# A fused transformer layer on one core: two additions and one subtraction move to GpSimd, two accumulators swap banks, and pieces of the order on TensorE, VectorE and ScalarE change

## The reference, cut to what matters

```python
y = layernorm(x)
y = LN1(y + causal_attention(y, y, y))         # one head, d = 256
y = LN2(y + attention(y, ctx, ctx))            # 64 context rows
ff = relu(y @ w1 + b1) @ w2 + b2               # 256 -> 1024 -> 256
x1 = x + LN3(y + ff)
n  = fp4(layernorm(x1))                        # blocks of 16: scale, round to the FP4 grid
h  = silu(n @ w_gate.T) * (n @ w_up.T)         # 256 -> 704, weights in fp4 too
x2 = x1 + fp4(h) @ w_down.T                    # 704 -> 256
```

## Time and profile before

| | before |
|---|---|
| median of 3 runs | 654.59 us (651.49 to 655.66) |
| the profiled execution | 656.84 us, of it the span from first to last instruction 655.0 us |
| PE busy | 587.8 us (90%) |
| PEld, weight loads beside PE | 549.1 us (84%) |
| DVE busy | 517.7 us (79%) |
| ACT busy | 381.8 us (58%) |
| POOL busy | 345.7 us (53%) |
| mean granted clock of TensorE | 0.963 of full speed |

### The profile page before, as it was taken

The page is one execution under the profiler, slowest core; times in us unless marked ns, Lnnn a source line. Parts: engine busy times, 40 slices in busy tenths (PEclk is TensorE's granted clock), DMA queues, the critical chain, the costliest instruction groups (busy, mean ns, idle before and its releaser), DMA issues.

```text
span 655.0 us, 12390 instructions
## 1 busy us (share of the span) xinstructions
PE 587.8 (90%) x4021; PEld 549.1 (84%) x4021; DVE 517.7 (79%) x1268; ACT 381.8 (58%) x781; POOL 345.7 (53%) x416
## 2 busy tenths in 40 slices
PE   4876769999999999999999999999999998989665
PEld 3765759898989898998989898989899898988665
DVE  3688677788778878888879878887879877988752
ACT  3456365575747666666657574766666664746331
POOL 2555363574646655565547554655556554654521
PEclk9977898999999999999999999999999999999887
DMA  7601000010100101010101010010101000000000
GB/s 226 203 2 32 2 13 30 0 50 1 33 26 10 42 1 58 0 48 0 56 0 41 7 32 24 0 48 0 56 2 33 2 32 2 18 1 17 9 9 16
DMA packets 18743, 19.30 MB, mean 29 GB/s; under 512 B 1537, under 2 KB 18193, under 8 KB 18705
## 3 DMA queue, kind: packets, MB, share of 16 engines
q1 hardware_dynamic: 18704, 18.82, 9.3%
HBM read 14.62 MB, written 4.19 MB: 29 GB/s over the span
## 4 chain that ended last, share of the span: by engine, by line
PE 60%; DVE 20%; issue 9%; ACT 5%; POOL 2%; DMA 1%; SPq 1%; DVEq 0%; ACTq 0%; POOLq 0%
PE O L964 4%; PE R L983 4%; PE R L916 4%; PE TR L804 4%; PE R L918 4%; PE O L1008 4%; PE R L917 4%; PE O L1029 3%; PE O L1027 3%; PE O L1028 3%; PE R L984 3%; PE R L985 3%; PE R L804 3%; PE O L1009 3%; PE O L1010 3%
## 5 line engine op out<-in xcount | busy, mean ns | idle before, releaser
L453 POOL TENSOR_TENSOR rs<-mv,neg_half 128x1 f32<-128x1 f32 (+1 forms) x112 | 69.5, 626 | 53.2 <-DVE mv L1250 51.8
L916 PE MATMUL R<-gu_hi,xqT_hi 128*128 128x352 f32 x256 | 87.2, 341 | 3.2 <-issue 2.2
L459 POOL TENSOR_TENSOR hs<-hh,h_rec 128x704 f32<-128x704 f32 x32 | 44.6, 1393 | 76.5 <-DVE h_rec L1286 76.5
L983 PE MATMUL R<-y2T_hi,w_hi 128*128 128x256 f32 x256 | 78.4, 306 | 7.2 <-DVE y2T_lo L1383 5.0
L918 PE MATMUL R<-gu_hi,xqT_lo 128*128 128x352 f32 x256 | 83.9, 328 | 0.0
L917 PE MATMUL R<-gu_lo,xqT_hi 128*128 128x352 f32 x256 | 83.9, 328 | 0.0
L670 ACT ACTIVATE hqT_hi<-R 128x768 fp32r<-128x768 f32 x32 | 26.0, 813 | 92.0 <-PE R L804 92.0
L1027 PE MATMUL O<-w_hi,hT_hi 128*128 128x256 f32 x256 | 73.9, 289 | 0.0
L985 PE MATMUL R<-y2T_hi,w_lo 128*128 128x256 f32 x256 | 72.6, 284 | 0.0
L984 PE MATMUL R<-y2T_lo,w_hi 128*128 128x256 f32 x256 | 72.6, 283 | 0.0
L1029 PE MATMUL O<-w_hi,hT_lo 128*128 128x256 f32 x256 | 72.5, 283 | 0.0
(11 more groups left out here) (146 smaller groups left out, 1804.2 us busy)
## 6 DMA issues: line engine op xcount, KB each, us to landing
x_in<-in_x SPq DMA_DIRECT2D x16, 256.0 KB, 2.7
x_res<-in_x SPq DMA_DIRECT2D x16, 256.0 KB, 2.7
out<-x SPq DMA_DIRECT2D x32, 128.0 KB, 1.7
ctx_rows<-in_ctx SPq DMA_DIRECT2D x16, 64.0 KB, 2.4
hT<-in_L_xattn_w SPq DMA_DIRECT2D x1, 1024.0 KB, 8.1
hh<-in_L_xattn_w SPq DMA_DIRECT2D x1, 768.0 KB, 8.0
wd_raw<-in_L_ffn_w_down SPq DMA_DIRECT2D x1, 704.0 KB, 8.3
w_raw<-in_L_ffn_w_gate SPq DMA_DIRECT2D x1, 640.0 KB, 4.5
```

The lines of the kernel that those rows point to most:

```text
L916: mm(o, xh, gu_hi[:, c, m, cols], start=(c == 0), stop=False)
L983: mm(o, w1_hi[:, c, cols], y2T_hi[:, c, :], start=(c == 0), stop=False)
```

## The change

1. `x1_sum` for both tiles leaves VectorE and stands on GpSimd right behind `gamma3` of its tile.
2. The last lower half of relu(h), j = 3, becomes `h_lower_last` on GpSimd, behind `scale_h(0)`; the second piece of `ff2` waits for its own semaphore.
3. The banks of `values`, `down`, `down_add`, `self_reciprocal` and `self_sum` are swapped: tile t uses `O[t]`. `values(0)` thus waits for `cross_sum` only, and `values(1)` for `ff_sum(1)`. `ff2` for t = 0 now waits for both `down_add`, of which the second moves forward on VectorE.
4. On TensorE `ff2` for t = 1 is cut: its first quarter (the bias and six matmuls) runs ahead of `turn_hq(0)`.
5. VectorE: `h_scale(1)` and `h_reciprocal(1)` ahead of `cross_sum`; `shift(2)`, `hT_lower(0)` and `shift(3)` of tile 0 ahead of `ff_sum(1)` (the latter two were first in the next slot); `cross_max` ahead of `h_lift(0)`; `self_reciprocal(1)`, `self_sum(1)` earlier.
6. ScalarE: the upper half of y2 turned comes ahead of `norm_x`.

```diff
@@ -244,6 +245,7 @@
         FF2_CUT = 5 * FC // 8
+        FF2_TURN = FC // 4
         FIRST = 3
@@ -483,6 +485,11 @@
+def h_lower_last(b, h):
+    wait(pool, h_hi_set, b, h, F, 4, 4)
+    pool.tensor_tensor(hT_lo[:, 6:8, :], hT[:, 6:8, :], hT_hi[:, 6:8, :].bitcast(F32),
+                       ALU.subtract).then_inc(h_lo_last, 1)
+
 def residual(b, h):
@@ -504,6 +511,7 @@
         gamma3(b, g, 0)
+        x1_sum(b, g, 0)
     if q1:
@@ -511,6 +519,7 @@
         gamma3(b, g, 1)
+        x1_sum(b, g, 1)
         unscale_x(b, g, 0)
@@ -536,6 +545,8 @@
         scale_h(b, h, 0)
+    if f:
+        h_lower_last(b, h)
     if a:
@@ -557,6 +568,13 @@
     pool.tensor_tensor(z3[:, t, :], z3[:, t, :], g3_row[:], ALU.mult).then_inc(y3_set, 1)
+
+def x1_sum(b, h, t):
+
+    wait(pool, y3_set, b, h, F, T, t + 1)
+    wait(pool, xb_set, b, h, F, T, t + 1)
+    wait(pool, x2_set, b, h, Q + 1, T, t + 1)
+    pool.tensor_tensor(x1[(h - F) % 2][:, t, :], z3[:, t, :], xb[:, t, :], ALU.add).then_inc(x1_set, 1)
@@ -724,14 +742,14 @@
         norm(3, b, g, F, 0, T, z3[:, 0, :], z3[:, 0, :])
-    if front:
-        norm_x(b, h)
     if f:
         if isinstance(b, int) and HALVES * b + h == F:
             act.wait_ge(b1_fold_set, 1)
         wait(act, n2_turned, b, h, F, 1, 1)
         act.activation(y2T_hi[:], TR[1][:].rearrange("p (c r) -> p c r", c=KC),
                        ACT.Copy).then_inc(y2T_hi_set, 1)
+    if front:
+        norm_x(b, h)
     if q1:
@@ -951,9 +969,9 @@
             wait_batch(pe, exp_full, b, 1, 0)
+        wait(pe, z2_set, b, h, F, T, T)
+    else:
         wait(pe, z3_set, b, h, F + 1, T, T)
-    else:
-        wait(pe, z2_set, b, h, F, T, T)
     lhs = []
@@ -961,7 +979,7 @@
     for i, (key, e) in enumerate(lhs):
-        last = mm(O[1 - t][:, 0:D + 1], e, y0[:, key, :], start=(i == 0), stop=(i == len(lhs) - 1))
+        last = mm(O[t][:, 0:D + 1], e, y0[:, key, :], start=(i == 0), stop=(i == len(lhs) - 1))
     last.then_inc(pv_done, 1)
@@ -1001,7 +1019,7 @@
     wait(pe, z1_set, b, h, A - 1, T, t + 1)
-    o = O[1 - t][:, 0:D]
+    o = O[t][:, 0:D]
     for i in range(IC):
@@ -1014,9 +1032,11 @@
         wait(pe, h_hi_set, b, h, F, 4, n)
-        wait(pe, h_lo_set, b, h, F, 4, n)
+        wait(pe, h_lo_set, b, h, F, 3, min(n, 3))
+        if n == 4:
+            wait(pe, h_lo_last, b, h, F, 1, 1)
         if fs[0] == 0:
-            wait(pe, x2_set, b, h, Q + 1, T, 1)
+            wait(pe, x2_set, b, h, Q + 1, T, T)
     else:
@@ -1037,7 +1057,7 @@
         wait_batch(pe, ctx_lo_set, b, 1, 1)
-    wait(pe, x2_set, b, h, Q + 1, T, T)
+    wait(pe, x2_set, b, h, Q + 1, T, 1)
     for t in range(T):
@@ -1124,12 +1144,14 @@
         cross_values(b, h)
+    if f:
+        ff2(b, h, 1, range(FF2_TURN))
     if q:
         turn_hq(b, h, 0)
     if front and h == 0:
         turn_context(b)
     if f:
-        ff2(b, h, 1, range(FC))
+        ff2(b, h, 1, range(FF2_TURN, FC))
     prepare(b, h, "end")
@@ -1339,7 +1361,7 @@
     store_wait(b, h, t)
-    v.tensor_tensor(x2[:, t, :], O[1 - t][:, 0:D], x1[(h - Q) % 2][:, t, :], ALU.add).then_inc(x2_set, 1)
+    v.tensor_tensor(x2[:, t, :], O[t][:, 0:D], x1[(h - Q) % 2][:, t, :], ALU.add).then_inc(x2_set, 1)
@@ -1347,13 +1369,8 @@
     wait(dve, y2_set, b, h, F, T, t + 1)
+    wait(dve, x1_set, b, h, F + 1, T, t + 1)
     v.tensor_tensor(z3[:, t, :], O[1][:, 0:D], y2[t][:], ALU.add).then_inc(z3_set, 1)
-
-def x1_sum(b, h, t):
-    wait(dve, y3_set, b, h, F, T, t + 1)
-    wait(dve, xb_set, b, h, F, T, t + 1)
-    i = (h - F) % 2
-    v.tensor_tensor(x1[i][:, t, :], z3[:, t, :], xb[:, t, :], ALU.add).then_inc(x1_set, 1)
@@ -1427,10 +1444,6 @@
     prepare(b, h, "early")
-    if q1:
-        hT_lower(b, g, 0)
-    if f1:
-        shift(3, b, g, F, (0,))
     if a:
@@ -1441,11 +1454,14 @@
     if f1:
-        x1_sum(b, g, 0)
+        z3_stats(b, g, 1)
         x1_stats(b, g, 0)
+        aggregate(3, b, g, F, 1)
         aggregate(4, b, g, F, 0)
-        z3_stats(b, g, 1)
-        aggregate(3, b, g, F, 1)
+    if a:
+        self_reciprocal(b, h, 1)
+        self_sum(b, h, 1)
+    if f1:
         x_norm(b, g, 0)
@@ -1453,14 +1469,10 @@
         hT_lower(b, g, 1)
-    if a:
-        self_reciprocal(b, h, 1)
-        self_sum(b, h, 1)
     prepare(b, h, "self")
     if f1:
         x_lift(b, g, 0)
         x_drop(b, g, 0)
-        x1_sum(b, g, 1)
         x1_stats(b, g, 1)
@@ -1476,6 +1488,8 @@
         xT_lower(b, h, 0)
+    if q1:
+        down_add(b, g, 1)
     if f1:
@@ -1502,10 +1516,6 @@
         h_product(b, h, 1, 0)
-    if f:
-        h_lower(b, h, (3,))
-    if q1:
-        down_add(b, g, 1)
     if front:
@@ -1514,11 +1524,11 @@
         h_product(b, h, 1, 1)
-        h_lift(b, h, 0)
     if a:
         cross_max(b, h)
     prepare(b, h, "cross")
     if q:
+        h_lift(b, h, 0)
         h_drop(b, h, 0)
@@ -1526,12 +1536,12 @@
         ff_sum(b, h, 0)
-    prepare(b, h, "late")
-    if a:
-        cross_sum(b, h)
     if q:
         h_scale(b, h, 1)
         h_reciprocal(b, h, 1)
+    prepare(b, h, "late")
+    if a:
+        cross_sum(b, h)
     if a:
@@ -1542,11 +1552,15 @@
         aggregate(3, b, h, F, 0)
+    if a:
+        shift(2, b, h, A, (0, 1))
+    if q:
+        hT_lower(b, h, 0)
+    if f:
+        shift(3, b, h, F, (0,))
         ff_sum(b, h, 1)
     if front:
         shift(0, b, h + 1, 0, (0, 1))
-    if a:
-        shift(2, b, h, A, (0, 1))
     prepare(b, h, "end")
```

13 lines of the change are left out of this document (7 added, 6 removed).

## The result

The changed kernel takes **634.07 us** (median of 4 runs, 633.72 to 635.11); the kernel before, run beside it, 655.12 (651.49 to 656.72). The ratio is 0.969, 95% interval 0.965 to 0.973. In a second measurement the same kernel took 636.28 (6 runs, 633.65 to 638.29), ratio 0.973 (0.970 to 0.976). The forecast of 642.3 had the direction right and was 8 us too high.

What follows compares the result with a forecast made beforehand. TensorE was taken as the bound. Terms 5.1 + 2.4 + 1.4 + 0.9 + 2.5 = 12.3 us came off the profiled 656.84, giving 644.5, then 642.3 for the median (profile 2.25 above it); range 636.5 to 650.

Steps and rivals of the forecast that it cites:

- What bounds it: Steady part: TensorE is the bound, busy 68.73 of 71 us; unchanged matmuls leave at most 2.3 us per 71, plus ramps.
- the three waits named for it: TensorE's steady waits: values for the second ff_sum 8.1 us, turn of ce 4.8, scores for hqT_lo 3.2.
- Term A: Slot boundary: swapped banks cut the stall before values; 3.6 us at even and 1.5 at odd slots, 5.1 in all.
- Term B: Ahead of the scores, odd slots: VectorE starts hqT_lo earlier; 6 x 0.4 = 2.4 us.
- Term C: Turn of ce and cross_values: odd slots win 0.3, even slots lose 0.1; 1.4 us in all.
- Term D: First slots: ScalarE's y2T_hi ahead of two norm_x starts about 0.9 us earlier; 0.9 us, bounds 0 and 1.1.
- Term E: Last slots: earlier norm 2 in slot 17 and earlier h_lift(1) into slot 18; 2.5 us, bounds 1.0 and 4.0.
- GpSimd's new work blocks VectorE: Rival: GpSimd's three new instructions per slot hold VectorE's two-input ones 0.7 to 1.1 us; 648.2 us, chance 0.10.
- VectorE late: Rival, slot's end: hT_lower(0) ahead of ff_sum(1) costs 0.5 instead of 0.15; 646.7 us, or 649; chance 0.16.
- ff2's second half stands for the first sum: Rival, slower: ff2's second half waits for ff_sum(0); each 0.1 us costs 1.6, 661.5 at 1.2 per slot; chance 0.07.
- All the waits go: Rival: TensorE's waits vanish, gaining 19 us (A 8.0, B 3, C 4, D 1, E 3); 635.6 us, chance 0.12.
- Moving 3 us of work off VectorE is worth nothing by itself: Claim on VectorE's load: with TensorE the bound, taking 3 us of work off VectorE alone gains nothing.

Runs made afterwards that it cites:

- e1: Changed kernel with ff2 for t = 1 not cut, h's first turn ahead of it again: 637.62 us, ratio 0.975.
- e7: Changed kernel with h_lift(0) ahead of cross_max again on VectorE: 633.74 us, ratio 0.967.
- e4: Kernel before with only the banks swapped and down_add(1) moved forward: 646.49 us, ratio 0.988.
- e6: Changed kernel with VectorE's old end-of-slot order (hT_lower(0), shift(3) after ff_sum(1), shift(2) last): 642.61 us, ratio 0.981.
- e12: Kernel before with only the banks swapped, down_add(1) forward and the two operations on GpSimd: 640.12 us, ratio 0.979.
- e5: Changed kernel with ScalarE's old order, norm_x ahead of the copy y2T_hi: 638.33 us, ratio 0.976.
- e3: Changed kernel with x1's sums and the last quarter of relu(h)'s lower part back on VectorE: 641.17 us, ratio 0.980.
- e11: Kernel before with only x1's sums and the last quarter of relu(h)'s lower part on GpSimd: 646.89 us, ratio 0.986.
- e2: Changed kernel with only the banks swapped back: 647.37 us, ratio 0.988.
- c3: Changed kernel with, in slot 3 only, ScalarE's relu(0, 1) ahead of the norm of z3's second half: 637.55 us, ratio 0.974.
- c4: Changed kernel with h_lift(0) ahead of cross_max and, in slot 3, relu(0, 1) ahead of z3's second norm, relu(2, 3) ahead of abs_x(1): 633.94 us, ratio 0.967.
- c5: c4 with VectorE's last two weight parts (wd_lo) in slot 3 ahead of the statistics of z1 and x: 633.13 us, ratio 0.968.
- e9: Kernel before with only ScalarE's new order, the copy y2T_hi ahead of norm_x: 651.62 us, ratio 0.996.

## Why the prediction was right or wrong

**What bounds it: right.** TensorE's 4021 matmuls stayed, the middle went to 98.8% busy, and each of the three waits named for it went. The sizes of the terms were off, all in one direction: 12.3 us were forecast and the two spans differ by 23.0. Of the 10.7 between, 3.5 are term A in the middle (0.59 a pair), some 1 are B and C there, 3.3 are slot 3 (term D, the clock below), 1.2 the end, 1.3 lie ahead of slot 3, and 0.4 are left over.

**Term A, mis-sized: the step that failed is what I took off it.** By the table the boundary gained 1.32 us a pair (6.79 + 8.00 to 6.26 + 7.21); the forecast had 0.73 (3.6 and 1.5 over seven boundaries each). Three parts of it:
- The cut of ff2, priced at 0.10 a slot, costs nothing: without it a pair is 0.02 longer (e1). I had read the 0.19 from ff2 to `cross_values` as the price of a change of kind. It was a wait: `cp_lower` ended at 360.85 + 0.43 = 361.28, and TensorE started 0.10 behind it; in e7 the same 0.10 stands between 419.89 and 419.99. In the changed kernel the bias matmul follows `cross_values` 0.12 later, and `values` follow ff2 0.11 later.
- With that, the stall in the even slot was worth more than 0.61: the first matmul of `values` stood 0.80 behind ff2 and stands 0.11 behind it, 0.69 earlier; the table says 0.79 with the banks. Where the last 0.1 comes from stays open.
- In odd slots I took 0.15 off since VectorE would be late with `ff_sum(1)` there. It is on time (PE, then DVE of after, an odd boundary):

```profile
353.97 0.28 PE L1049 MATMUL O<-w_hi,hT_lo 128*128 128x256 f32 x1
354.09 0.59 PE L982 MATMUL O<-y,e_diag 128*128 128x257 f32 x2
```

```profile
353.22 0.95 DVE L1357 TENSOR_TENSOR hqT_lo<-R,hqT_hi 128x768 fp32r<-128x768 f32 x1
...
354.29 0.42 DVE L1373 TENSOR_TENSOR w_raw<-O,b_row 128x256 f32<-128x256 f32 x1
```

The sum starts 0.32 behind the start of ff2's last matmul, just as far as the first sum in the earlier trace rows (361.51 against 361.19), so the 1.07 us of work put ahead of it (353.22 to 354.29) filled VectorE's idle time and no more. And the new order also put `shift(2)` first, which ended the 0.2 us waits of z2's turn for its norm that stand in e4, e6 and e12. A loss of 0.15 was forecast, a gain of 0.37 measured (6.63 to 6.26, banks and operations to after).

**Term B, right in size.** 0.48 a pair (14.83 to 14.35) against 0.4. The operations off VectorE's queue gave 0.38 alone (14.45). The banks alone cost 0.14 here (14.97), and two orders win as much back, VectorE's at the slot's end 0.07 (e6) and ScalarE's 0.08 (e5), the latter not in the forecast. With the operations undone (e3) the piece stays at 14.36, so either edit ends this wait by itself.

**Term C, right in sum, wrong in both parts.** I had 0.3 won in odd slots by `cross_max` and 0.1 lost in even ones. The turn of ce gained 0.83 a pair, and e11 shows that the two operations do that with `cross_max` at its old place. With the operations there, `cross_max` ahead of `h_lift(0)` only made `cp_lower` late, by 0.33 a slot. (Without them, in e3, the move does it alone, at a later `cp_lower` still.) Net 0.28 against 0.2 a pair. I had named the very chain (`h_lift`, `h_drop`, `h_max`, `cp_lower`) and priced its shift at 0.1. The move was not needed beside the operations: ScalarE's table load set the start of the exponentials, with `cross_max` 0.08 ahead of it (e7).

**Term D, the wait near, the slot not: the step that failed is TensorE's clock, which the forecast put at nothing.** The wait for `y2T_lo` in slot 3 fell from 2.8 to 1.5, 1.3 where 0.9 was forecast and 1.1 was the bound. But the slot gained 4.2. Its mean clock went from 0.89 to 0.96; times the length that is 45.29 x 0.11 = 5.0 us short of full clock before and 41.11 x 0.04 = 1.6 after. So by this estimate up to 3.4 of the 4.2 came from the clock, which fell once instead of twice, and about 0.8 from waiting. Over all kernels of this study slot 3 took 40.6 to 45.3 us, with a mean clock of 0.88 to 0.96. e5, e6, e7, e2 and c3, with quite different edits, all lose 1.8 to 2.9 there. e7 shows it best: TensorE's waits in its slot 3 are those of the changed kernel to 0.1 us (3.4 for `e_full`, 2.0, 1.5 for `y2T_lo`), and the slot takes 43.89 at a mean clock of 0.88, 2.8 more (windows view; beside it stands the row 73.82:114.93 above):

```profile
73.30:117.19 43.89, 36.26 (x226) 34.23 (x225) 32.62 (x77) 23.92 (x49) 25.84 (x30) 0.88 0.06 16
```

That is why its undos don't add up. Nor does ScalarE's new order carry the slot: e12 has the old order and a wait of 2.9 for `y2T_lo`, and its slot 3 takes 41.07. What decides whether the clock falls once or twice stays open. In c3, c4 and c5 the longer waits, 9.0, 8.7 and 7.0 us in sum, go with the lower clock, 0.88, 0.92 and 0.96; e7, whose edit stands far from slot 3 in the program, waits no longer than the changed kernel and has the lower clock all the same.

**Term E, near.** 4.6 against 3.4 with the rest of A and C. The wait of z2's turn in slot 17 fell from 1.77 to 0.92, 0.85 where 0.9 was forecast. Ahead of slot 18 the distance from `h_lift(0)` to `h_lift(1)` fell from 8.45 (603.24 to 611.69) to 7.24 (583.20 to 590.44), 1.2 where 1.6 was forecast. The mean clock of the end went from 0.90 to 0.92, 106.7 x 0.10 = 10.7 to 102.1 x 0.08 = 8.2 us short of full clock, which can be up to 2.5 of the 4.6. e9 with one order of ScalarE changed won 2.4 there at 0.93, e6 lost 4.6 at 0.88: here too an undo measures the clock as much as its edit.

**GpSimd and VectorE.** POOL's busy time rose by 36.7 us (41 forecast). The new operations are 46.6, longer than forecast (`x1_sum` 0.78 instead of 0.73, the subtraction 1.36 instead of 1.1), and the others lost 10, most of it the rows of y2 and y1, 966 to 734 ns each. DVE fell by only 23 (45 forecast). The groups of after:

```profile
L577 POOL TENSOR_TENSOR w_raw<-w_raw 128x256 f32<-128x256 f32 x32 | 24.9, 778 | 2.8 <-POOL w_raw L570 0.6
L490 POOL TENSOR_TENSOR hT_lo<-hT,hT_hi 128x512 fp32r<-128x512 f32 x16 | 21.7, 1358 | 0.0
L1341 DVE SCALAR_TENSOR_TENSOR xa<-xa,wd_raw 128x256 f32<-128x256 f32 x32 | 20.2, 631 | 1.1
...
L1430 DVE SCALAR_TENSOR_TENSOR ctx_lo<-ctx_vals,ctx_hi 128x256 fp32r<-128x256 f32 x8 | 9.6, 1196 | 0.0
```

and of the kernel before:

```profile
L1330 DVE TENSOR_TENSOR hT_lo<-hT,hT_hi 128x512 fp32r<-128x512 f32 x64 | 59.4, 929 | 1.2 <-ACT hT_hi L665 1.1
L1319 DVE SCALAR_TENSOR_TENSOR xa<-xa,wd_raw 128x256 f32<-128x256 f32 x32 | 13.6, 425 | 1.1
L1413 DVE SCALAR_TENSOR_TENSOR ctx_lo<-ctx_vals,ctx_hi 128x256 fp32r<-128x256 f32 x8 | 4.0, 495 | 0.0
```

`x_drop` went from 425 to 631 ns: 16 of its 32 lie beside a new `x1_sum` on GpSimd and take up to 0.85 us, and with the operations undone (e3) all are at 425 again. `ctx_lower` went from 495 to 1196, but most of that is old work that came to lie beside it: of the 9.6 us of its eight, 7.2 lie beside `scale_h` and 2.3 beside the new subtraction, and in e3 they take 744 ns. So the rival "GpSimd's new work blocks VectorE", for which the prediction had named the Trainium skill's rule on two SBUF inputs (SBUF — State Buffer, Who interferes with whom), was right about the mechanism and wrong about the price: no wait of TensorE for these stands in the middle, while `h_lower(3)`, which was removed, stood ahead of `cp_lower`.

**The other rivals.** *VectorE late* did not come, as the rows above show. *ff2's second half stands for the first sum* happened once, at the end, for 0.8 us. *All the waits go* comes nearest, 635.6, and what I had set against it ("`values(0)` of odd slots is too short") did not bind: no matmul of `values` waits in the changed kernel. But its number is in part luck. It had 4 us for C, where 0.28 a pair makes 2.0 over seven, and 1 for D, where slot 3 gained 4.2 by the clock.

**"Moving 3 us of work off VectorE is worth nothing by itself": wrong**, the sentence furthest from the runs. Alone it is worth 1.38 us a pair and 8 us of the whole (e11: 646.89 against 655.02).

## What to carry to other kernels

Price a moved piece of work by what stands behind it in its queue, not by its engine's load: two sums and a subtraction taken out of the queue ahead of late links were worth more alone (1.38 us a pair) than the bank swap alone (1.02), on an engine that was not the bound. An order that pays beside one edit (`hT_lower(0)` ahead of the sum, 0.5 us a pair with the banks swapped) costs three times as much without it (1.6). So try parts alone as well as undone; the two prices of one part differed by up to four times here. And judge a ramp with idle stretches by its granted clock before crediting an edit: compare kernels by the steady pair first, where two executions agreed to 0.01 us, and look at each pair before taking the mean.

## What the hardware showed that I had not expected

- A change between matmuls of differing operands and banks costs nothing when nothing is late: 0.11 to 0.12 us between starts, as within a run (ff2 to `values`, 388.46 to 388.57; `cross_values` to the bias, 384.84 to 384.96). The distance of 0.19 in the earlier trace rows, with no idle time printed beside it, was a wait.
- Of TensorE's clock: behind waits of 4.1 and 2.0 us in slot 3 of c3 it stood at 0.50 and 0.52 in two windows of five, the second full of work, before it was at 1.00 again; with the same waits in slot 3 two kernels differed there by 2.8 us (after and e7); 1.7 us less of waiting went with 2.6 us less time (c4 to c5); and one kernel's timed runs spread by 4.6 us, with mean clocks from 0.956 to 0.970.
- The contention of VectorE and GpSimd moved with the work: it more than doubled `ctx_lower` (495 to 1196 ns) and added half to `x_drop` (425 to 631), and a pair was not longer for it (69.16 with x1's sums on GpSimd; undoing them beside the subtraction added nothing, 69.53 against 69.56).
